# Two later attentions of a transformer stack: four heads' maxima at once, the division on VectorE, tiles interleaved

## The reference, cut to what matters

```python
q = jnp.einsum('bsc,hcd->bhsd', xn, wq)
k = jnp.einsum('btc,hcd->bhtd', yn, wk)
v = jnp.einsum('btc,hcd->bhtd', yn, wv)
a = jax.nn.softmax(jnp.einsum('bhsd,bhtd->bhst', q, k) * D ** (-0.5), axis=-1)
if causal:
    s, t = (a.shape[-2], a.shape[-1])
    mask = (jnp.arange(t)[None, :] > jnp.arange(s)[:, None]).astype(a.dtype)
    a = a * mask
o = jnp.einsum('bhst,bhtd->bhsd', a, v)
```

## Time and profile before

| | us |
|---|---|
| median of 3 timed runs | 3877.21 (3872.72 to 3889.8) |
| span of the profiled execution | 3882.5 |
| PE busy in the span | 3392.2 (87%) |
| DVE busy | 2480.8 (64%) |
| ACT busy | 1950.3 (50%) |
| POOL busy | 1423.1 (37%) |
| mean granted clock of TensorE | 0.917 |

### The profile page before, as it was taken

How to read it: one execution, slowest core, us unless ns; L and a number is a source line. 1 busy time by engine, 2 the same in 40 slices (tenths; PEclk the granted TensorE clock), 3 DMA queues, 4 the chain that set the end, 5 groups by cost and what they waited for, 6 DMA issues and landing times. The chain is left out here.

```text
span 3882.5 us, 65515 instructions
## 1 busy us (share of the span) xinstructions
PE 3392.2 (87%) x22711; PEld 1574.6 (41%) x22711; DVE 2480.8 (64%) x4757; ACT 1950.3 (50%) x3913; POOL 1423.1 (37%) x719
## 2 busy tenths in 40 slices
PE   5999999725994899999999986899999998969998
PEld 2333333414773233333332264233333232657776
DVE  5877687374114778777787355777777772555665
ACT  2777777421112257566666733255555555423443
POOL 2000000253222241434226140366666666505553
PEclk7999899866997799999999887799999999969999
DMA  1000000177772100100000030100000000437445
GB/s 58 11 15 10 13 6 6 66 271 257 229 241 91 33 13 9 25 6 17 17 9 5 1 107 23 39 14 17 14 15 14 8 9 1 130 112 258 93 83 116
DMA packets 163212, 239.02 MB, mean 62 GB/s; under 512 B 35859, under 2 KB 132826, under 8 KB 155994
## 3 DMA queue, kind: packets, MB, share of 16 engines
q1 hardware_dynamic: 142698, 209.40, 16.9%
q0 software_dynamic: 19056, 24.88, 3.5%
q10 hardware_dynamic: 1152, 0.79, 0.1%
HBM read 136.44 MB, written 68.92 MB: 53 GB/s over the span
## 5 line engine op out<-in xcount | busy, mean ns | idle before, releaser
L1266 DVE TENSOR_REDUCE a_part_max<-a_wb 128x1 f32<-128x512 f32 (+1 forms) x2048 | 1162.0, 625 | 232.3 <-PE a_wb L1338 221.7
L1218 ACT ACTIVATE a_e<-a_sc 128x512 f32<-128x512 f32 (+1 forms) x1472 | 795.2, 599 | 693.2 <-PE a_sc L1372 686.3
L1177 POOL TENSOR_TENSOR a_part_sum<-a_part_sum,a_e 128x2048 f32<-128x2048 f32 x160 | 724.6, 4528 | 103.3 <-ACT a_e L1218 87.1
L1338 PE MATMUL a_wb<-a_ks,a_qs 96*128 96x512 f16 (+1 forms) x2048 | 738.9, 372 | 26.5 <-DVEq L1246 9.5
L1372 PE MATMUL a_sc<-a_qs,a_ks 97*128 97x512 f16 (+1 forms) x1472 | 545.7, 384 | 11.7 <-DMA a_qs<-a_neg_max 8.1
L757 DVE TENSOR_REDUCE xa_part_max<-xa_mx 128x2 f32<-128x802 f32 x512 | 471.4, 986 | 128.1 <-PE xa_mx L864 125.4
L693 ACT ACTIVATE xa_e<-xa_sc 128x512 f32<-128x512 f32 (+1 forms) x832 | 445.6, 597 | 130.2 <-PE xa_sc L851 122.7
L1338 PEld LDWEIGHTS a_wb<-a_ks,a_qs 96*128 96x128 f16 x2048 | 200.6, 98 | 620.6 <-DVE a_part_max L1266 451.6
L1395 PE MATMUL a_po<-a_e,a_v 128*32 128x512 f32 (+1 forms) x2432 | 324.0, 605 | 1.9 <-ACT a_dc L1189 1.0
L1166 POOL TENSOR_TENSOR a_em<-a_e,a_later 128x512 f32<-128x512 f32 x64 | 80.9, 1265 | 579.1 <-issue 365.8
L887 PE MATMUL xa_po<-xa_e,xa_v 128*32 128x256 f32 (+1 forms) x3328 | 269.5, 396 | 7.5 <-ACT xa_oc L743 2.6
(11 more groups left out here) (362 smaller groups left out, 4589.5 us busy)
## 6 DMA issues: line engine op xcount, KB each, us to landing
experts_w_up<-in_we SPq DMA_DIRECT2D x32, 1024.0 KB, 6.5
wall<-expert_halves SPq DMA_DIRECT2D x18, 1088.0 KB, 7.1
experts_w_down<-in_we SPq DMA_DIRECT2D x32, 512.0 KB, 6.0
a_qs<-a_stage SPq DMA_DIRECT2D x360, 32.0 KB, 1.9
moe_xr<-sorted_rows SPq DMA_DIRECT2D x79, 136.5 KB, 2.1
a_ks<-a_stage SPq DMA_DIRECT2D x336, 32.0 KB, 1.9
choose_whole<-in_wm SPq DMA_DIRECT2D x18, 544.0 KB, 9.0
expert_halves<-choose_cut SPq DMA_DIRECT2D x18, 544.0 KB, 8.3
```

What stands on the lines that cost most here:

```text
L1177: pool.tensor_tensor(part_sum[:, :, :], part_sum[:, :, :], tile, ALU.add).then_inc(pool_added, 1)
L1218: act.activation(e[:r, m % ering, j, :], sc[(HG * m + j) % NSC][:r, :], ACT.Exp, scale=scale).then_inc(exp_done, 1)
L1266: dve.tensor_reduce(part_max[:, j, t, k:k + 1], src[:, :mxw], AX.X, ALU.max).then_inc(unit_taken, 1)
L1338: last = pe.matmul(dst[:, :mxw], qs[:STACK, j, n % NQ, P * t:P * t + P], ks[:STACK, g % 2, j, mxs[k]:mxs[k] + mxw], start=True, stop=True)
```

## The change

`attention_stacked` is replaced by `attention_quad` for a1 and a2.

- **Maxima**: of the high halves alone, which have 32 rows. Four matmuls on four row groups make those of four heads for 128 queries and 512 keys (a **quad**), into `mx`, four banks that exist once. DVE takes two heads in each of two reductions. The next quad's first two heads wait for the first reduction, the others for the second. A block has 16 quads in a1 and 13 in a2 (the last with 65 keys).
- **PSUM**: four banks `mx`, one `po`, one `pd`, and so two `sc` (`NSC = 2`). The projections and the turns go through this ring of two too, and ACT takes them. POOL splits q and k.
- **Heads on rows**: three heads use 97 rows, the fourth 128, with zeros.
- **Order of a tile**: two scores, the quad, the values of the tile before, directly behind them the sum of its weights, two scores, a projection. Of a shared tile the values come in two halves of 256 columns, the second behind the later scores.
- **Shared tiles**: in a2, 5 in a block, and 8 weighed. In a1 8, 5, 3 and 0 in blocks 0 to 3.
- **Interleaving** (a1): passed tiles stand evenly between the others.
- **Division**: DVE transposes the divisors in 32 x 32 blocks, inverts, transposes back and multiplies. PE has only four small matmuls left in a1 (`carry`), for the passed tiles' sums.
- **Constants** of POOL are set ahead of the first turn and not at the start.

```diff
-    NST = 3
-    NQ = 3
-    NWB = 3 if ones_at is None else 4
-    NSC = 3
-    PASSED_WORK, TILE_WORK = 5, 8
-    LEAD = 2
+    NST, NQ, NR, NSC = 3, 3, 1, 2
+    LEAD = 4
...
+    def on_pool(n, kt):
+
+        i = kt - first_kept(n)
+        if kt >= nkt - 2 or i <= 0 or nkt - first_kept(n) <= TPC:
+            return False
+        if not causal:
+            return kt % 2 == 1
+        return i >= TPC and i % 4 != 3 if n % NCH == 0 else i % 2 == 1
...
+        tiles += sorted(((n, kt) for kt in range(nkt)),
+                        key=lambda x: (2 * x[1] + 1) * kept if x[1] < skipped else (2 * (x[1] - skipped) + 2) * skipped)
...
+        order += scores[:2] + maxima[:1]
+        order += [("pv", last_n, last_k, 0, parts)] if kept else []
+        order += [("sum", last_n, last_k)] if weighed else []
+        order += scores[2:] + lone.get(m, [])
+        order += [("pv", last_n, last_k, 1, parts)] if parts == 2 else []
+        order += maxima[1:]
...
+                for t in (i % TPC,) if i < TPC * nfull else range(TPC):
+                    for j in range(HG):
+                        if m and j % 2 == 0:
+
+                            pe.wait_ge(m_taken, 2 * m - 1 + j // 2)
+                        rows = slice(SLOT * j, SLOT * j + SLOT)
...
+            for u in order:
+                if u in s_at and s_at[u] >= NSC:
+
+                    pe.wait_ge(s_taken, s_at[u] - NSC + 1)
...
+                elif u[0] == "norm":
+                    n = u[1]
+                    dve.wait_ge(o_taken, 2 * (n + 1))
+                    dve.transpose(tr[:, :], dc[:, :]).then_inc(norm_step, 1)
```

More of the change, by code:

```diff
@@ L1028, in attention_stacked, with put @@
+    order += [("rowmax", 0), ("turn", 0)]
+    wide, lone = {}, {}
+    def put(n, slot, *units):
+        m = nkt * n + slot - LEAD
+        lone.setdefault(max(m, 0), []).extend(units)
     for n in range(NC):
         g, qc = n // NCH, n % NCH
-        work = []
-        if g + 1 < NG:
[L1032 to L1058, removed]
+        if n + 1 < NC:
+            for i, u in enumerate(quads(n + 1)):
+                wide.setdefault(nkt * n + i - LEAD if n else i * (nkt - LEAD) // nkt, []).append(u)
+            put(n, nkt, ("turn", n + 1))
@@ new lines, in attention_quad @@
+    for m in range(nkt * NC + 1):
+        n, kt = tiles[m] if m < nkt * NC else (NC, 0)
+        last_n, last_k = tiles[m - 1]
+        scores = [("s", n, kt, j) for j in range(HG)] if n < NC else []
+        kept = m and not passed(last_n, last_k)
+        weighed = kept and not on_pool(last_n, last_k)
+        parts = 1 if weighed or not kept or diagonal_of(last_n, last_k) is not None else 2
+        maxima = wide.get(m, [])
+        order += scores[:2] + maxima[:1]
[4 more added lines that the diff above has]
+        order += maxima[1:]
+        if maxima and maxima[-1][2] == nquad - 1:
+            order.append(("rowmax", maxima[-1][1]))
+        if 0 < n and m == nkt * n:
+            order.append(("out", n - 1))
@@ new lines, in attention_quad @@
+    if passed(NC - 1, 0):
+        order += [("total", NC - 1), ("carry", NC - 1)]
+    order.append(("norm", NC - 1))
+    s_at = {u: i for i, u in enumerate(u for u in order if u[0] in ("k", "q", "v", "s", "turn", "carry"))}
+    quad_at = {u: i for i, u in enumerate(u for u in order if u[0] == "max")}
+    staged = {u: i for i, u in enumerate(u for u in order if u[0] in ("k", "q"))}
+    pv_at = {u[1:3]: i for i, u in enumerate(u for u in order if u[0] == "pv" and u[3] == u[4] - 1)}
+    sum_at = {u[1:3]: i for i, u in enumerate(u for u in order if u[0] == "sum")}
@@ L1446, in _ @@
-            for u in after:
-                unit(u)
+                    last = pe.matmul(pd[h:h + SLOT, :], ones[:r, :SLOT], e[:r, m % ering, j, :], start=(kt == first), stop=(kt == last_kt))
+                last.then_inc(sum_done, 1)
+            for u in order:
+                if u in s_at and s_at[u] >= NSC:
+                    pe.wait_ge(s_taken, s_at[u] - NSC + 1)
+                if u[0] in ("k", "q", "v"):
+                    project(u)
+                elif u[0] == "s":
+                    score(u)
+                elif u[0] == "max":
+                    quad(u)
+                elif u[0] == "pv":
+                    sum_values(u)
+                elif u[0] == "sum":
+                    sum_weights(u)
+                elif u[0] == "turn":
+                    pe.wait_ge(rowmax_ready, u[1] + 1)
+                    pe.transpose(sc[s_at[u] % NSC][:HG * TPC, :P], row_max[:, :, :].rearrange("p j t -> p (j t)"),
+                                 a["ident"][:, :]).then_inc(s_ready, 1)
+                elif u[0] == "carry":
+                    pe.wait_ge(blocks_ready, carry_at[u[1]] + 1)
+                    pe.wait_ge(fold_made, 1)
+                    for j in range(HG):
+                        h = SLOT * j
+                        last = pe.matmul(sc[s_at[u] % NSC][h:h + SLOT, :HG * TPC], fold[:, :], by_block[:, j, :, :].rearrange("p t u -> p (t u)"),
+                                         start=True, stop=True)
+                    last.then_inc(s_ready, 1)
```

567 lines of the change are left out of this document (293 added, 274 removed).

## The result

The changed kernel takes 4083.5 us (median of 5 runs, 4075.1 to 4104.4) against 3877.2 (5 runs): 1.053 times as long, interval 1.050 to 1.056, 206 us more. The forecast was 92 more. The profiled execution, the slowest of the five, has a span of 4102.3 us, 219.8 over the one before.

| stretch | before, us | after, us | difference | forecast |
|---|---|---|---|---|
| up to a1's first projection of k | 1244.9 | 1258.0 | +13 | 0 |
| from there to the first exponential, a1; a2 | 71.4; 60.2 | 83.6; 67.7 | +12; +8 | +10 together |
| a1, first to last exponential | 915.0 | 1080.3 | +165 | +47 and +33 for the clock |
| a2, the same | 796.0 | 839.4 | +43 | +22 |
| tails, a1; a2 | 16.7; 21.6 | 8.7; 6.3 | -8; -15 | -20 together |

What follows compares the result with a forecast made beforehand. PE's issue was taken to bound a2, and a1 outside its passed tiles. a2 22, a1 47, run-up 10, tails -20 and clock 33 sum to 92 over 3877: 3970 us, range 3850 to 4090.

Steps and rivals of the forecast that it cites:

- Ring of two: Two score banks, each turning round in 1.07 us: 4.1 us a weighed tile, 0.9 of it PE waiting; 2.8 a shared one.
- The quad's 0.32: PE's time for four packed maxima matmuls, taken at the price of two packed ones in layer 0, with 512 columns for 401.
- other estimate of 0.29: Quad's time on PE from the skill's speedup of 3.07 for four matmuls; said to change the sum by 0.04 a tile.
- The clock: Half clock in a1's passed tiles: 0 to 142 us, taken as 33, about 8 a block 3.
- rival 2: Half clock through a1's blocks 2 and 3 costs 142 us for 33, so 4080 us in all; chance 0.15.
- The prediction's own sign of being wrong: Wrong if a1's clock falls through whole groups, a weighed a2 tile takes 3.2 us, or PE waits little for exponentials.
- The maxima banks: `mx` exists once, so quad to quad takes 2.8 us; held to bound passed tiles alone, 0.6 each for quads right behind.
- a1's table: Times of a1's four blocks by tile kind, with projections, division and copies added: 962 us at full clock, 47 more.
- Run-up: Ahead of each attention's first exponential: maxima, q's copies and POOL's row of ones, bounded by 0 and 12, 10 together.
- Tails: Behind each attention's last exponential: one division left, without PE, 9 us for 16.7 and 21.6, giving back 20.
- The division: On DVE some 2.5 us a block, hidden where a weighed tile follows; 5 added in a1 with ACT's copies.

Runs made afterwards that it cites:

- half reductions: The changed kernel with DVE's reductions over the first half of each maxima bank alone, leaving out the maxima of half of the keys: 3973.9 us.
- filler: The changed kernel with matmuls added that change no result, where PE waits for a bank or a mask: 4074.8 us.
- sum_in_gap: The changed kernel with the sum of a tile's weights again behind the third and fourth score, not directly behind the values: 3954.4 us.

## Why the prediction was right in direction and short in size

- **Ring of two: right.** 4.1 and 2.8 us a tile and 1.07 a turn were found to 0.02. Moving one sum won back 0.7 of the 0.9 us that PE was to wait in a weighed tile. The quad's 0.32 was found too (0.39 in the tile shown); the prediction's other estimate of 0.29 is 0.03 a tile below it, not 0.04.
- **The clock: the step that failed.** "if half of each three and the kept tile behind run at half clock [...] I take 33." That puts half clock behind the passed tiles of block 3 alone. It came in all blocks, even in blocks 0 without a passed tile, and cost a1 some 67 us, at least 50: by the estimate, 34 of the 85 us that a1 came out over the forecast. The argument against rival 2, that kept tiles with PE's densest work stand between the passed ones, fell: PE waits for banks, masks and reductions in kept tiles too. The prediction's own sign of being wrong, a clock that falls through whole groups, came true. That the median lies within 4 us of rival 2's 4080 is luck: rival 2 has 142 us of half clock and none of the parts below.
- **The maxima banks: the turn right, their part too small.** A quad's turn was 2.84 us for 2.8. The table had some 29 us for them in a1 (0.6 a quad behind a passed tile, and block 3's 2.8 for 2.4); near full clock they are worth 41. Nothing was put down for the first block of either attention, where some tiles have two quads. In a2 this, and the half clock that goes with it, make the first block 16 us longer than the next, most of the 21 that a2 came out over the forecast. In a1 it is 6 us longer than the next group's, and 1.5 with half reductions.
- **a1's table besides: open.** At filler's clock and without its added matmuls a1 would be some 1031 - 18 = 1013 us against 962 forecast; 12 of these 51 are the reductions. The cause of the other 39 stays open. What the 88 us of half clock left in filler cost is among them, and no run parts that from masks, projections and the starts of blocks.
- **Run-up: 20 and not 10.** With half reductions it was 73.8 and 63.0 in place of 83.6 and 67.7, so DVE's reductions make most of it.
- **Tails: right.** 23 given back for 20 forecast; 9 forecast, 8.7 and 6.3 found. The tail of a1, which answers to the earlier trace rows:

```profile
2421.29 0.60 ACT L1247 ACTIVATE a_e<-a_sc 128x512 f32<-128x512 f32 x1 [0.20 <-PE a_sc L1394]
...
2430.63 1.62 PE L1540 MATMUL a_out_y<-a_wo,a_ot 128*128 128x256 f32 x3 [3.64 <-PEq L1076]
```

- **The division: priced by its instructions alone.** In the changed kernel its product took up to 2.3 us, usually 0.7, and in sum_in_gap 4.5 in three blocks of a1. What such a wait for POOL costs was measured in the old order only.

Against the 92: 85 more in a1, 21 in a2, 10 in the run-ups, 13 ahead of a1, 3 less for tails and 2 for the rest make the 128 by which the two profiled spans differ from the forecast.

## What to carry to other kernels

A ring with one bank fewer costs little where long matmuls stand between two uses of a bank (some 40 us here, in the old order), and much where the uses follow each other, so order the work for the ring before counting the time that PE saves. When a change leaves PE waiting often, price every tile at both clocks, not only those with the least work. Before moving elementwise work to DVE, look at where both operands lie and what POOL does then.

## What was not expected of the hardware

Matmuls that do nothing paid for themselves in a1: 758 more instructions on PE, and 50 us less. And a reduction cut to half its columns gave back twice what its waits cost near full clock (82 us against 41): a1's half clock fell from 374 us to 210 with it.
